# A Mamba block with a routed expert layer: the first group's silu, W_xproj product and first softplus piece done chunk by chunk, z evacuations placed behind

## The reference, cut to what matters

```python
h = _L0_tok_ref(x, W_embed, b_embed, W_proj, b_proj)      # conv + patch projection -> (64, 128, 256)
h = h + _L0_attn_ref(_layernorm(h), ...)                  # the selective-scan block
h = h + _L0_ffn_ref(_layernorm(h), ...)                   # 8 experts, top 2

def _forward(x, W_in, conv_w, conv_b, W_xproj, w_dt, b_dt, A_log, D_param, W_out):
    x_inner, z = jnp.split(x @ W_in, 2, axis=-1)
    xc = silu(depthwise_conv4(x_inner) + conv_b)
    x_ssm = xc @ W_xproj                                  # 33 columns: delta_raw, Bm (16), Cm (16)
    delta = jax.nn.softplus(x_ssm[..., :1] * w_dt + b_dt)
    y = _selective_scan(xc, delta, -jnp.exp(A_log), Bm, Cm)   # h = exp(delta*A)*h + delta*Bm*xc; y = h.Cm
    y = (y + xc * D_param) * jax.nn.silu(z)
    return y @ W_out
```

## Time and profile before

| what | value |
|---|---|
| median of three runs (lowest to highest) | 2898.72 us (2897.68 to 2898.99) |
| profiled execution, its own time | 2897.52 us |
| its span | 2895.8 us |
| PE busy | 2564.7 us (89%) |
| DVE busy | 2097.2 us (72%) |
| ACT busy | 1476.2 us (51%) |
| POOL busy | 1730.1 us (60%) |

### The profile page before, as it was taken

The page is one execution under the profiler, slowest core; times in us unless marked ns, Lnnn a source line. Parts: engine busy times, 40 slices in busy tenths (PEclk is TensorE's granted clock), DMA queues, the critical chain, the costliest instruction groups (busy, mean ns, idle before and its releaser), DMA issues. The chain is left out here.

```text
span 2895.8 us, 29805 instructions
## 1 busy us (share of the span) xinstructions
PE 2564.7 (89%) x7998; PEld 1279.0 (44%) x7999; DVE 2097.2 (72%) x2271; ACT 1476.2 (51%) x2733; POOL 1730.1 (60%) x864
## 2 busy tenths in 40 slices
PE   4589898988989989889898898976499999999999
PEld 2134343343433434334343343432266666666665
DVE  0399999999999999999999999999322222222222
ACT  1566766667666676666766667664122222222222
POOL 1467787787887878878778787786222222222222
PEclk9799999999999999999999999999699999999999
DMA  1303314133141331413304133031522222222221
GB/s 40 133 34 112 122 38 145 57 118 128 32 145 63 112 129 31 146 63 112 134 28 145 69 105 136 23 138 58 195 46 43 44 44 44 44 45 43 45 45 29
DMA packets 125604, 236.15 MB, mean 82 GB/s; under 512 B 46449, under 2 KB 93714, under 8 KB 109122
## 3 DMA queue, kind: packets, MB, share of 16 engines
q1 hardware_dynamic: 98342, 200.56, 20.2%
q0 software_dynamic: 26128, 34.36, 6.9%
q10 hardware_dynamic: 1036, 0.09, 0.0%
HBM read 182.22 MB, written 53.78 MB: 81 GB/s over the span
## 5 line engine op out<-in xcount | busy, mean ns | idle before, releaser
L515 POOL TENSOR_TENSOR arena<-u,arena 128x2048 f32<-128x2048 f32 x256 | 1160.0, 4531 | 351.8 <-DVE psum L914 348.6
L914 DVE TENSOR_TENSOR_SCAN psum<-psum,arena 128x1024 f32<-128x1024 f32 x512 | 1171.3, 2288 | 62.3 <-ACT psum L707 34.4
L1295 PE MATMUL psum<-hc,ident 128*128 128x512 f32 x2048 | 1003.9, 613 | 238.1 <-DVE hc L922 237.7
L1295 PEld LDWEIGHTS psum<-hc,ident 128*128 128x128 f32 x2048 | 356.5, 191 | 751.9 <-DVE hc L922 468.6
L707 ACT ACTIVATE psum<-delta,a_neg 128x508 f32<-128x508 f32 x1024 | 656.5, 674 | 0.6
L922 DVE TENSOR_TENSOR hc<-psum,arena 128x1024 f32<-128x1024 f32 x512 | 624.8, 1220 | 9.9
L590 POOL DMA_INDIRECT out_dram<-hres,tok_id x136 | 211.8, 1557 | 598.7 <-ACT hres L849 545.2
L1429 PE MATMUL psum<-arena,xnt 128*128 x1088 | 515.6, 596 | 0.0
L1181 DVE COPY z<-psum 128x512 f32<-128x512 f32 x136 | 94.1, 692 | 458.1 <-PE psum L1438 458.1
L849 ACT ACTIVATE hres<-psum,tok_w 128x256 f32<-128x256 f32 x136 | 64.5, 474 | 454.4 <-PE psum L1448 447.7
L1448 PE MATMUL psum<-arena,z 128*128 x1088 | 257.1, 379 | 0.9 <-DVE z L1181 0.9
(11 more groups left out here) (144 smaller groups left out, 1952.2 us busy)
## 6 DMA issues: line engine op xcount, KB each, us to landing
arena<-ssm_rows SPq DMA_DIRECT2D x128, 1024.0 KB, 5.8
delta<-expert_rows SPq DMA_DIRECT2D x136, 129.0 KB, 2.1
h_saved_rows<-hnew SPq DMA_DIRECT2D x16, 512.0 KB, 6.7
hres<-h_saved_rows SPq DMA_DIRECT2D x16, 512.0 KB, 3.5
out_dram<-h SPq DMA_DIRECT2D x16, 512.0 KB
draw<-ssm_rows SPq DMA_DIRECT2D x16, 256.0 KB, 3.3
arena<-in_L_ffn_wg_dram SPq DMA_DIRECT2D x8, 512.0 KB
arena<-in_L_ffn_wi_dram SPq DMA_DIRECT2D x8, 512.0 KB
```

The lines of the kernel that those rows point to most:

```text
L515: pool.tensor_tensor(dBx[k % 2], rep, b_rep[:, q * QN:(q + 1) * QN, :], ALU.mult).then_inc(dbx_ready, 1)
L914: nc.vector.tensor_tensor_scan(h, h, src, 0.0, ALU.mult, ALU.add).then_inc(scan_done, 1)
L1295: last = nc.tensor.matmul(yacc[(k // HC) % 2], ident[:, :], hc[k % 2][:, i, :], start=False, stop=(k % HC == HC - 1 and i == 1))
```

## The change

Only group 0 is concerned. ACT applies silu straight from the convolution's bank, chunk by chunk (`conv_silu_first`), and PE multiplies chunk c-1 by its part of W_xproj behind the convolution of chunk c, into a bank of its own, 7 (`x_ssm_first`). Softplus runs first for chunk 0 alone; Abs of the other chunks comes behind the first relu and one z evacuation, their Exp behind `exps(0,0)`, their Ln into step 3, their relus into steps 3 to 5. The z evacuations of chunks 1 and 2 move behind `exps(0,0)` and into step 0. POOL splits the first dBx in two halves, and its add and u for chunks 1 and 2 move from behind dBx(1) and dBx(4) to behind dBx(3) and dBx(5). The semaphore `abs_ready` counts one less in the first group, so `softplus_exp` waits for one less.

```diff
@@ -167,6 +167,7 @@
         yacc = [psum[:, 4, :], psum[:, 7, :]]
         bank_a, bank_b = psum[:, 5, :], psum[:, 6, :]
         emb_pair = [bank_a, bank_b]
+        ssm_bank = psum[:, 7, :]
 
         def scratch(i):
             return bank_b[:, (2 + i) * GB * E:(3 + i) * GB * E].rearrange("p (b e) -> p b e", b=GB)
@@ -215,6 +216,7 @@
         conv_full = sem("conv_full")
         conv_done = sem("conv_done")
         xc_ready = sem("xc_ready")
+        xc_first = sem("xc_first")
         z_full = sem("z_full")
         z_free = sem("z_free")
         z_ready = sem("z_ready")
@@ -227,6 +229,10 @@
         abs_ready = sem("abs_ready")
         sexp_ready = sem("sexp_ready")
         ln_ready = sem("ln_ready")
+        abs_first = sem("abs_first")
+        sexp_first = sem("sexp_first")
+        ln_first = sem("ln_first")
+        dbx_first = sem("dbx_first")
         relu_ready = sem("relu_ready")
         delta_ready = sem("delta_ready")
         u_ready = sem("u_ready")
@@ -493,7 +499,9 @@
                     .then_inc(done, 1)
 
             def add_delta(g, c):
-                if c == 0:
+                if g == 0 and c == 0:
+                    pool.wait_ge(ln_first, 1)
+                if c == (1 if g == 0 else 0):
                     pool.wait_ge(ln_ready, g + 1)
                 pool.wait_ge(relu_ready, NCH * g + c + 1)
                 pool.tensor_tensor(delta[:, c, :], delta[:, c, :], soft[:, c, :], ALU.add).then_inc(delta_ready, 1)
@@ -511,6 +519,11 @@
                 if c == 0:
                     pool.wait_ge(b_loaded[q], 16 * (g + 1))
                 ahead(pool, scan_done, HU * g + 2 * k - 2)
+                if g == 0 and k == 0:
+                    two = u[:, 0, :].rearrange("p (a t) -> p a t", a=1).broadcast_to([P, 2, GT])
+                    pool.tensor_tensor(dBx[0][:, 0:2, :], two, b_rep[:, 0:2, :], ALU.mult).then_inc(dbx_first, 1)
+                    pool.tensor_tensor(dBx[0][:, 2:4, :], two, b_rep[:, 2:4, :], ALU.mult).then_inc(dbx_ready, 1)
+                    return
                 rep = u[:, c, :].rearrange("p (a t) -> p a t", a=1).broadcast_to([P, QN, GT])
                 pool.tensor_tensor(dBx[k % 2], rep, b_rep[:, q * QN:(q + 1) * QN, :], ALU.mult).then_inc(dbx_ready, 1)
 
@@ -547,8 +560,8 @@
                     make_dbx(g, k)
                     if k == 0 and not last:
                         rsqrt(g + 1, 0, stat1, pow1)
-                    if k in (1, 4, 8):
-                        c = {1: 1, 4: 2, 8: 3}[k]
+                    if k in ((3, 5, 8) if first else (1, 4, 8)):
+                        c = {1: 1, 3: 1, 4: 2, 5: 2, 8: 3}[k]
                         add_delta(g, c)
                         make_u(g, par, c)
                     if not second:
@@ -651,6 +664,40 @@
                     ahead(actq, u_ready, NCH * (g - 1))
                 nc.scalar.activation(xc[par][:, c, :], bank, ACT.Identity, bias=cb[:, c:c + 1]).then_inc(conv_done, 1)
 
+            def conv_silu_first(c, bank):
+                actq.wait_ge(conv_full, c + 1)
+                done = xc_ready if c == NCH - 1 else xc_first
+                nc.scalar.activation(xc[0][:, c, :], bank, ACT.Silu, bias=cb[:, c:c + 1]).then_inc(conv_done, 1)
+                actq.wait_ge(conv_done, c + 1)
+                actq.sem_inc(done, 1)
+
+            def evac_ssm_first():
+                actq.wait_ge(ssm_full, 1)
+                nc.scalar.activation(ssm_sb[:, :], ssm_bank[0:R, :], ACT.Copy).then_inc(ssm_done, 1)
+
+            def softplus_first():
+
+                actq.wait_ge(draw_loaded, 16)
+                nc.scalar.activation(soft[:, 0, :], draw[:, :], ACT.Abs, scale=wdt[:, 0:1], bias=bdt[:, 0:1])\
+                    .then_inc(abs_first, 1)
+                actq.wait_ge(abs_first, 1)
+                nc.scalar.activation(soft[:, 0, :], soft[:, 0, :], ACT.Exp, scale=-1.0).then_inc(sexp_first, 1)
+                actq.wait_ge(sexp_first, 1)
+                nc.scalar.activation(soft[:, 0, :], soft[:, 0, :], ACT.Ln, bias=1.0).then_inc(ln_first, 1)
+                softplus_relu(0, 0)
+                evac_z(0, 0)
+                for c in range(1, NCH):
+                    nc.scalar.activation(soft[:, c, :], draw[:, :], ACT.Abs, scale=wdt[:, c:c + 1],
+                                         bias=bdt[:, c:c + 1]).then_inc(abs_ready, 1)
+
+            def softplus_exp_rest():
+                actq.wait_ge(abs_ready, NCH - 1)
+                nc.scalar.activation(soft[:, 1:, :], soft[:, 1:, :], ACT.Exp, scale=-1.0).then_inc(sexp_ready, 1)
+
+            def softplus_ln_rest():
+                actq.wait_ge(sexp_ready, 1)
+                nc.scalar.activation(soft[:, 1:, :], soft[:, 1:, :], ACT.Ln, bias=1.0).then_inc(ln_ready, 1)
+
             def silu_x(g, par):
                 actq.wait_ge(conv_done, NCH * (g + 1))
                 nc.scalar.activation(xc[par], xc[par], ACT.Silu).then_inc(xc_ready, 1)
@@ -669,7 +716,7 @@
                     .then_inc(abs_ready, 1)
 
             def softplus_exp(g):
-                actq.wait_ge(abs_ready, NCH * (g + 1))
+                actq.wait_ge(abs_ready, NCH * (g + 1) - 1)
                 nc.scalar.activation(soft[:, :, :], soft[:, :, :], ACT.Exp, scale=-1.0).then_inc(sexp_ready, 1)
 
             def softplus_ln(g):
@@ -746,21 +793,13 @@
                 for c in range(NCH):
                     if c + 1 < NCH:
                         evac_xi(0, c + 1, emb_pair[(c + 1) % 2])
-                    evac_conv(0, 0, c, emb_pair[c % 2])
-                silu_x(0, 0)
-                evac_ssm(0)
+                    conv_silu_first(c, emb_pair[c % 2])
+                evac_ssm_first()
                 for m in range(2):
                     evac_xt(1, m)
                 for m in range(2):
                     evac_h(1, m)
-                for c in range(NCH - 1):
-                    evac_z(0, c)
-                for c in range(NCH):
-                    softplus_abs(0, c)
-                softplus_exp(0)
-                softplus_ln(0)
-                for c in range(NCH):
-                    softplus_relu(0, c)
+                softplus_first()
 
             def step(g, par, first, second, more, last):
                 for k in range(HU):
@@ -769,6 +808,12 @@
                     elif not last:
                         softplus_relu(g + 1, 3)
                         exps(g + 1, 0)
+                    if first and k == 3:
+                        softplus_ln_rest()
+                    if first and k in (3, 4, 5):
+                        softplus_relu(0, k - 2)
+                    if first and k == 0:
+                        evac_z(0, 2)
                     if not last and k in (1, 2):
                         norm1(g + 1, k - 1)
                     if k == 2:
@@ -825,6 +870,8 @@
             front()
             actq.wait_ge(s_diag, N_DIAG + 1)
             exps(0, 0)
+            softplus_exp_rest()
+            evac_z(0, 1)
             steps(step, tail)
 
 
@@ -907,7 +954,9 @@
             def scan(g, k):
 
                 dve.wait_ge(dA_ready, HU * g + k + 1)
-                if k % 2 == 0:
+                if g == 0 and k == 0:
+                    dve.wait_ge(dbx_first, 1)
+                elif k % 2 == 0 or (g == 0 and k == 1):
                     dve.wait_ge(dbx_ready, UN * g + k // 2 + 1)
                 h = flat(dA[k % 2])
                 src = flat(dBx[(k // 2) % 2][:, 2 * (k % 2):2 * (k % 2) + 2, :])
@@ -1275,6 +1324,18 @@
                                             start=(c == 0), stop=(c == NCH - 1))
                 last.then_inc(ssm_full, 1)
 
+            def x_ssm_first(c):
+                if c == 0:
+                    pe.wait_ge(s_wts, 16 * N_WTS)
+                if c < NCH - 1:
+                    pe.wait_ge(xc_first, c + 1)
+                else:
+                    pe.wait_ge(xc_ready, 1)
+                last = nc.tensor.matmul(ssm_bank[0:R, :], w_x[:, c, :], xc[0][:, c, :],
+                                        start=(c == 0), stop=(c == NCH - 1))
+                if c == NCH - 1:
+                    last.then_inc(ssm_full, 1)
+
             def project_z(g, c, embedded):
 
                 if c == 0:
@@ -1355,8 +1416,9 @@
                         project_x_first(c + 1)
                     conv(0, c, 0, emb_pair[c % 2])
                     conv(0, c, 1, emb_pair[c % 2])
-                pe.wait_ge(s_wts, 16 * N_WTS)
-                x_ssm(0, 0)
+                    if c > 0:
+                        x_ssm_first(c - 1)
+                x_ssm_first(NCH - 1)
                 for m in range(2):
                     turn_x(1, m)
                 for m in range(2):
```

## The result

The changed kernel took 2876.37 us (median of 6 runs, 2875.21 to 2878.46) against 2896.84 us for the kernel before (6 runs, 2895.53 to 2898.99): a ratio of 0.9929 with a 95% interval of 0.9916 to 0.9942, or 20.5 us less. Forecast were 2875.8 us and a gain of 22.9 us. The profiled execution of the changed kernel is the longest of its six, 2878.46 us; that of before was above the median too, 2897.52.

What follows compares the result with a forecast made beforehand. DVE, pausing little once scans start, was taken as the bound, so an earlier first scan counts: 7.6 + 11.5 + 4.7 + 2.0 − 1.4 − 1.5 = 22.9 us, giving 2875.8 us. Range 2871 to 2881, to 2884 with most cold-PE cases.

Steps and rivals of the forecast that it cites:

- part 1: Convolution, silu and W_xproj projection of group 0: ssm_sb done at 76.1 us instead of 83.74, 7.6 us saved (bounds 5.5 to 8).
- part 2: Start of softplus: Abs 6.7 us after ssm_sb, no longer behind three z evacuations; 11.5 us saved.
- part 3: First piece of softplus, from Abs to POOL's add: 5.5 us instead of 10.2, 4.7 us saved.
- part 4: From POOL's add to the first scan, with dBx split: 2.0 us saved, first scan at 93.6 us.
- 5a: POOL's second dBx half, group 1's rsqrt and dBx(1) make scan 2 wait 1.4 us, returning most of the split's gain.
- 5b: ACT in step 3, with the two added table loads, makes scan 5 wait 1.5 us.
- The first rival: PE is cold when the z projections come in group 0: some 8 us given back, time 2884; chance 12%.
- the sum of 20 us by that page: Total saving if each of the two added table switches also cost a drain, giving back another 2.8 us.
- 5c to 5f: Group 0's later ACT work before scan 1, moved add and u, broadcasts, and z projections: no cost expected.
- 5f's condition: The 3 z projections stay hidden in ACT's shadow if PE is at full clock by the third.
- a sign of being wrong: PE passes of 0.85 us or more behind 100 us would make the prediction wrong.
- 20 us lost in each 25: Rival that TensorE stays at its lower clock and becomes the bound: +70 over the first group, near 2945; chance 2%.

## Why the prediction was right

The direction, the chain and the time held: 2876.4 us measured, 2875.8 forecast, in the range of 2871 to 2884. That the time fits to 0.6 us is in part luck. The gain was forecast 2.4 us too large (22.9, measured 20.5), and it was taken from the 2898.7 us of three runs, while the six runs of before have a median of 2896.84; from there the same sum would give 2873.9. Point by point, with the two profiles of the changed kernel:

| step | forecast | first profile | second profile |
|---|---|---|---|
| ssm_sb done (part 1) | 76.1 | 77.83 | 76.01 |
| from there to Abs (part 2) | 6.7 | 7.7 | 8.2 |
| from Abs to POOL's add (part 3) | 5.5 | 5.5 | 5.5 |
| from the add to the first scan (part 4) | 5.3 | 5.15 | 5.14 |
| wait for POOL ahead of scan 2 (5a) | 1.4 | 1.70 | 1.70 |
| wait for ACT ahead of scan 5 (5b) | 1.5 | 1.18 | 1.18 |
| group 0 behind step 8, ahead of before | 22.9 | 20.18 | 21.45 |

*Part 1* was right: from the start of the convolution to ssm_sb it is 23.2 us in both profiles of the changed kernel and 30.6 in that of before, 7.35 us less for the 7.6 of the forecast. It has one gap: the W_xproj passes cost in the trace of before what the clock happened to be, and 6.43 us were taken as the price where another execution has 4.92. Against that one part 1 saves 5.8 us.

*Part 2 was mis-sized.* It held that draw's landing and the embedding's end, at the same moment before, would move together. Draw does (it lands 6.5 us after ssm_sb in the first profile), the embedding doesn't: with PE's clock lower it ends 7.8 and 8.3 us after ssm_sb where before it took 6.6, and Abs waits for it. This is not the chance of one execution: it is 8.3 us in every other kernel with the new convolution and no fillers, and 6.6 to 7.4 us in the four profiles with the old one. Fillers that keep the clock at its full level bring Abs back to draw's landing and 2.0 us of time, which shows the cause. The first rival had seen a cold PE, but placed it at the z projections and priced it at 8 us; there it cost nothing that can be seen. z(0,2) held ACT for 2.42 us (101.74 in the ACT rows), beside POOL's longer way to scan 2: with fillers ACT stands only 0.79 us there, and DVE's wait ahead of scan 2 is 1.71 us all the same.

*Parts 3 and 4* were right within 0.2 us, and so was 5a's remark that the split returns most of what it gives: 0.4 us are left of 2.1. *5b*: 1.18 us for 1.5. The Trainium skill, "ScalarE: Activation LUTs", section "What ACT_TABLE_LOAD costs", has some 1.38 us of drain with each load; an estimate from that page for this wait is some 4 us. This trace does not agree: it has 1.18 us, and Ln follows its load by 0.01 us (109.91 + 1.28, then 111.20). So the sum of 20 us by that page, though nearer to the measured 20.5, does not explain it. *5c to 5f* cost nothing, as forecast: no wait for a broadcast, for u or for dBx(4) is in the rows of DVE. But 5f's condition did not hold: the third z projection ran at the lower level (3.61 us, and 3.78 in the second profile), and in the second profile the pair by diag_d at 100.39 took 1.91 us, which is over the 0.85 us a pass that the prediction named as a sign of being wrong. The sign came and the cost didn't: add_state ran at the full clock right behind it (1.88 us for four passes in the first profile, 2.03 in the second).

Two figures beside the sum don't follow from their terms: the added bounds of 2.1, 1.3 and 2.6 us give 2881.8, not 2881, and 20 us lost in each 25 over a group of 117 us would be 94 us, not 70. Neither bears on the result.

That the early start stays to the end was right as well: DVE's last gate product of group 0 is 20.62 us ahead (242.25 before, 221.63 now), the last but four of the whole run 20.70 (1922.95 and 1902.25). The span of the first profile is only 19.1 us shorter (2895.8 and 2876.7), because the wait for the scattered rows behind the last group was 1.1 us longer in it (20.96 us ahead of the first expert tile against 19.81); in the second profile it is 19.86 and the span 21.8 shorter. That part is chance.

Of the 2.4 us between the forecast gain and the measured one, 1.0 to 1.5 us are the embedding's clock in part 2. For the rest the profile of before is the likely source: its front was slow where the change takes work away. From the start of the convolution to scan 9 the kernel before takes 97.5 and 94.7 us in its two profiles, the changed one 75.8 and 76.4. The gain is thus 18.3 to 21.6 us, depending on which two are compared, and 20.5 lies between. How often an execution of before has the one front or the other was not measured, so this part is not shown.

## What to carry to other kernels

When two events end together in a trace, ask of each what sets its length before moving both by the same amount: here one was a DMA, the other short matmuls whose price depended on what PE did before them. Removing an idle stretch of an engine can move its clock's low phase onto other work: here from W_xproj behind a wait of 4.09 us to the embedding of the next group. A wait that an edit adds can lower it too, as the later xnt evacuation did. And a few matmuls without a use in the waits, shorter than the waits, can be worth more than the next reordering (2.0 us here, against 1.1 for the later relus). Last, an early start at half a buffer only pays as far as the second buffer follows as early: the producer's other work, here the rsqrt, has to move behind it.

## What was not expected of the hardware

The same program shows PE at either clock level in the same place in different executions: eight passes of W_xproj took 6.43 and 4.92 us in two profiles of before, the second z projection 3.78 and 1.98 us, and in the changed kernel 3.69 us (at 91.43 in the first profile) and 1.98 us (at 90.16 in the second). The medians of before agree within 0.1% all the same (2895.92 to 2896.84 us over the sets), as the 2.7 us by which the two fronts differ are themselves less than 0.1% of the time. A price taken from one profile of such a stretch can be off by as much as these pairs.
